# Moving a bias addition from VectorE to GpSimd, and the order of VectorE's work, in the stage between two layers

## The reference

```python
x = x + attn0(xn0) + ffn0(xn0)            # ffn0: u + routed top-2 of 16 experts + shared
xn = (x - mean(x)) / sqrt(var(x) + 1e-5)  # _layernorm, over the last axis, 256 long
# attn1 starts with an rms norm of xn, times sqrt(256), times (gamma + 1)
x = x + attn1(xn) + (xn @ (ternary(weight) * alpha).T + bias)
```

## Time and profile before

| | before |
|---|---|
| median of 3 runs | 3188.59 us (3183.55 to 3188.95) |
| profiled execution | 3183.55 us, span 3181.5 us |
| busy over the span | PE 89%, DVE 68%, POOL 66%, ACT 60% |
| `settle` | 695.6 us (first load issued) to 943.3 us (first instruction of the next stage) |
| L1040 of the first and of the last unit | 707.2 and 928.0 us |

### The profile page before, as it was taken

How to read it: one execution, slowest core, us unless ns; L and a number is a source line. 1 busy time by engine, 2 the same in 40 slices (tenths; PEclk the granted TensorE clock), 3 DMA queues, 4 the chain that set the end, 5 groups by cost and what they waited for, 6 DMA issues and landing times.

```text
span 3181.5 us, 49742 instructions
## 1 busy us (share of the span) xinstructions
PE 2845.0 (89%) x14674; PEld 2191.7 (69%) x14674; DVE 2166.3 (68%) x3533; ACT 1899.3 (60%) x2746; POOL 2093.5 (66%) x1314
## 2 busy tenths in 40 slices
PE   5888848864448999999999999999999999999997
PEld 5788847753335677777777777777777777777775
DVE  7888843338876667677667667676676667667673
ACT  4555422222226777677777777677776777777774
POOL 4777741017744777777777777777777777777775
PEclk8988859985558999999999999999999999999998
DMA  3332125558871222222222232222222232232221
GB/s 120 107 107 89 62 83 163 179 180 264 258 228 43 60 56 69 55 65 73 43 76 55 61 76 48 69 54 69 54 64 73 44 76 57 60 76 50 69 53 46
DMA packets 266850, 281.11 MB, mean 88 GB/s; under 512 B 96754, under 2 KB 205554, under 8 KB 266739
## 3 DMA queue, kind: packets, MB, share of 16 engines
q1 hardware_dynamic: 254452, 246.17, 29.2%
q0 software_dynamic: 12288, 33.57, 3.5%
HBM read 129.67 MB, written 82.31 MB: 67 GB/s over the span
## 4 chain that ended last, share of the span: by engine, by line
PE 66%; DMA 1%; ACT 1%; DVE 1%; POOL 1%; issue 1%; SPq 0%; POOLq 0%; ACTq 0%; DVEq 0%
PE psV_b L1615 7%; PE psV_b L1610 7%; PE psV_b L1611 7%; PE psS_b L1598 7%; PE psS_b L1597 7%; PE psN_b L1583 7%; PE psY_b L1538 4%; PE psX_b L1538 4%; PE psY_b L1539 4%; PE psY_b L1540 4%; PE psX_b L1539 4%; PE psX_b L1540 4%; DMA xT_lo<-xT_lo_dram 1%; POOL pp_lo_b L1328 1%; PE psN_b L1667 0%
## 5 line engine op out<-in xcount | busy, mean ns | idle before, releaser
L1328 POOL TENSOR_TENSOR pp_lo_b<-pf_b,pp_hi_b 128x1024 fp32r<-128x1024 f32 x512 | 1228.7, 2400 | 609.0 <-ACT pp_hi_b L1370 523.0
L1474 DVE TENSOR_REDUCE negmax_b<-psN_b 128x2 fp32r<-128x1024 f32 x512 | 627.0, 1225 | 378.6 <-PE psN_b L1583 371.1
L1365 ACT ACTIVATE pf_b<-psS_b 128x1024 f32<-128x1024 f32 x512 | 525.8, 1027 | 238.7 <-PE psS_b L1598 235.6
L1597 PE MATMUL psS_b<-qA_b,kA_b 128*128 128x512 f32 x1024 | 405.9, 396 | 6.7 <-DVE qB_b L1489 4.8
L1598 PE MATMUL psS_b<-qB_b,kB_b 68*128 68x512 f32 x1024 | 406.3, 397 | 0.0
L1611 PE MATMUL psV_b<-pp_hi_b,vals_lo_b 128*64 128x512 f32 x1024 | 403.4, 394 | 0.0
L1610 PE MATMUL psV_b<-pp_hi_b,vals_hi_b 128*65 128x512 f32 x1024 | 401.8, 392 | 1.5
L1583 PE MATMUL psN_b<-kA_b,qA_b 128*128 128x512 f32 x1024 | 322.6, 396 | 4.6 <-DVE negmax_b L1474 4.5
L1389 ACT ACTIVATE kA_b<-psX_b 64x512 fp32r<-64x512 f32 x256 | 151.7, 593 | 290.1 <-PE psX_b L1540 285.2
L1615 PE MATMUL psV_b<-pp_lo_b,vals_hi_b 128*65 128x512 f32 x1024 | 320.2, 394 | 5.0 <-POOL pp_lo_b L1328 5.0
L1370 ACT ACTIVATE pp_hi_b<-pf_b 128x1024 fp32r<-128x1024 f32 x256 | 271.5, 1061 | 8.1
(11 more groups left out here) (246 smaller groups left out, 6542.4 us busy)
## 6 DMA issues: line engine op xcount, KB each, us to landing
kA_b<-kA_b SPq DMA_DIRECT2D x128, 256.0 KB, 3.2
qB_b<-qA_b SPq DMA_DIRECT2D x128, 256.0 KB, 2.9
inverse_b<-inverse_dram SPq DMA_DIRECT2D x256, 128.0 KB, 3.1
xs_e<-rows_dram SPq DMA_DIRECT2D x144, 128.0 KB, 2.1
results_dram<-ys_e SPq DMA_DIRECT2D x72, 256.0 KB, 2.4
x_a<-x_dram SPq DMA_DIRECT2D x16, 512.0 KB, 4.2
part_dram<-acc_a SPq DMA_DIRECT2D x32, 256.0 KB
acc_s<-part_dram SPq DMA_DIRECT2D x32, 256.0 KB
```

What stands on the lines that cost most here:

```text
L1328: pool.tensor_tensor(pp[1][:, c], pf[:, c], pp[0][:, c].bitcast(F32), ALU.subtract).then_inc(pl_pool, 1)
L1365: a.activation(pf[:, c], psS[:], ACT.Exp).then_inc(exp_act, 1)
L1474: v.tensor_reduce(negmax[:, n.slot(2), 2 * c:2 * c + 2], psN[:], AX.X, ALU.max, negate=True).then_inc(mx_dve, 1)
L1597: pe.matmul(psS[:, t], kA[:, s, keys], qA[:, s], start=True, stop=False)
```

## The change

Three things change in `settle`. The bias addition (result `x1b`) is executed by POOL instead of DVE, after the roots and before the gathers of each unit; the wait for the load of the bias moves from DVE to POOL. POOL computes the two roots in two power instructions of two elements each instead of one of four, and the second reads the variance directly, so that eps is added to two elements only. On DVE `rows_low` is merged into `finish`, which stands where `rows_low` stood: the subtraction, the wait for PE and the base rows of unit u - 1 now come ahead of the factors of unit u. The semaphore counts follow: `SD` is 15 instead of 16, `SP` 4 instead of 2.

```diff
@@ POOL
+            g.wait_ge(const_in, 16)
             for u in range(NU):
                 need(g, s_dve, SD, u, 9)
                 need(g, s_dve, SD, u - 2, SD)
-                g.tensor_tensor(vs[:, u % 2], mv[:, u % 2, :, 1].unsqueeze(1).to_broadcast([P, 2, U]), eps[:], ALU.add).then_inc(s_pool, 1)
+                g.tensor_tensor(vs[:, u % 2, 0], mv[:, u % 2, :, 1], eps[:], ALU.add).then_inc(s_pool, 1)
                 need(g, s_pool, SP, u, 1)
-                g.tensor_tensor(flat2(root[:, u % 2]), flat2(vs[:, u % 2]), flat2(power[:]), ALU.pow).then_inc(s_pool, 1)
+                g.tensor_tensor(root[:, u % 2, 0], vs[:, u % 2, 0], power[:, 0], ALU.pow).then_inc(s_pool, 1)
+                g.tensor_tensor(root[:, u % 2, 1], mv[:, u % 2, :, 1], power[:, 1], ALU.pow).then_inc(s_pool, 1)
+                need(g, o_dve, U, u - 3, U)
+                g.tensor_tensor(x1b[:, u % 3], x1[:, u % 3], fbias_bc[:].unsqueeze(1).to_broadcast([P, U, D]),
+                                ALU.add).then_inc(s_pool, 1)
                 gather(u + 3)
@@ DVE
-            def rows_low(u):
+            def finish(u):
                 if u < 0:
                     return
                 need(v, t_act, 1, u, 1)
+                v.tensor_tensor(flat(xrt[1][:, u % 2]), psT[:, u % 2], flat(xrt[0][:, u % 2]).bitcast(F32),
+                                ALU.subtract).then_inc(t_dve, 1)
+                need(v, s_pool, SP, u, 4)
                 if u >= 2:
                     v.wait_ge(stored[u % 2], 80 * (u // 2))
-                v.tensor_tensor(flat(xrt[1][:, u % 2]), psT[:, u % 2], flat(xrt[0][:, u % 2]).bitcast(F32),
-                                ALU.subtract).then_inc(t_dve, 1)
-
-            def finish(u):
-                if u < 0:
-                    return
                 need(v, f_pe, 1, u, 1)
                 for t in range(U):
                     v.scalar_tensor_tensor(out=base[:, u % 2, t], in0=psF[:, u % 2, t * D:(t + 1) * D], scalar=fac[:, u % 3, 5, t:t + 1],
                                            in1=x1b[:, u % 3, t], op0=ALU.mult, op1=ALU.add).then_inc(o_dve, 1)
 
-            v.wait_ge(const_in, 16)
             for u in range(NU):
...
                     v.bn_aggr(mv[:, u % 2, t], stats[:, u % 2, t]).then_inc(s_dve, 1)
-                rows_low(u - 1)
-                v.tensor_tensor(x1b[:, u % 3], x1[:, u % 3], fbias_bc[:].unsqueeze(1).to_broadcast([P, U, D]),
-                                ALU.add).then_inc(s_dve, 1)
+                finish(u - 1)
                 f = fac[:, u % 3]
-                need(v, s_pool, SP, u, 2)
+                need(v, s_pool, SP, u, 3)
                 v.tensor_tensor(f[:, 0], root[:, u % 2, 0], root[:, u % 2, 1], ALU.mult).then_inc(s_dve, 1)
...
                 v.scalar_tensor_tensor(out=f[:, 4], in0=mv[:, u % 2, :, 0], scalar=-1.0, in1=f[:, 3],
                                        op0=ALU.mult, op1=ALU.mult).then_inc(s_dve, 1)
-                finish(u - 1)
-            rows_low(NU - 1)
             finish(NU - 1)
```

More of the change, by code:

```diff
@@ L906, in settle @@
         power = sb("power", [P, 2, U])
-        eps = sb("eps", [P, 2, U])
+        eps = sb("eps", [P, U])
         acc = sb("acc", [P, 4, U, D])
@@ L927, in settle @@
             "const_in", "const_pool", "s_dve", "s_pool", "x_act", "t_pe", "t_act", "t_dve", "f_pe", "o_dve"))
-        SD = 5 + 2 + 2 + 1 + 6
-        SP = 2
+        SD = 5 + 2 + 2 + 6
+        SP = 4
         def flat(ap):
             return ap.rearrange("p a b c -> p (a b c)")
-        def flat2(ap):
-            return ap.rearrange("p a b -> p (a b)")
         block = ctx.enter_context(nc.Block())
@@ L977, in _ @@
         def _(g):
-            for tile, value in ((power[:, 0], -0.5), (power[:, 1], 0.5), (eps[:, 0], 1e-5), (eps[:, 1], 0.0)):
+            for tile, value in ((power[:, 0], -0.5), (power[:, 1], 0.5), (eps[:], 1e-5)):
                 g.memset(tile, value).then_inc(const_pool, 1)
-            g.wait_ge(const_pool, 4)
+            g.wait_ge(const_pool, 3)
             def gather(u):
@@ L1039, in _ @@
                 need(v, x_act, U, u - 3, U)
+                need(v, s_pool, SP, u - 3, 4)
                 v.tensor_tensor(acc[:, u % 4], acc[:, u % 4], x[:, u % 4], ALU.add).then_inc(s_dve, 1)
@@ L1054, in _ @@
                 need(v, s_dve, SD, u, 7)
-                need(v, s_pool, SP, u - 2, 2)
+                need(v, s_pool, SP, u - 2, 3)
                 for t in range(U):
                     v.bn_aggr(mv[:, u % 2, t], stats[:, u % 2, t]).then_inc(s_dve, 1)
-                rows_low(u - 1)
-                v.tensor_tensor(x1b[:, u % 3], x1[:, u % 3], fbias_bc[:].unsqueeze(1).to_broadcast([P, U, D]),
-                                ALU.add).then_inc(s_dve, 1)
+                finish(u - 1)
                 f = fac[:, u % 3]
-                need(v, s_pool, SP, u, 2)
+                need(v, s_pool, SP, u, 3)
                 v.tensor_tensor(f[:, 0], root[:, u % 2, 0], root[:, u % 2, 1], ALU.mult).then_inc(s_dve, 1)
+                need(v, s_dve, SD, u, 10)
+                v.tensor_scalar(f[:, 1], f[:, 0], 1e-12 * float(D) ** -0.5, None, ALU.max).then_inc(s_dve, 1)
                 need(v, s_dve, SD, u, 11)
-                v.tensor_scalar(f[:, 1], f[:, 0], 1e-12 * float(D) ** -0.5, None, ALU.max).then_inc(s_dve, 1)
-                need(v, s_dve, SD, u, 12)
                 v.reciprocal(f[:, 2], f[:, 1]).then_inc(s_dve, 1)
                 v.tensor_scalar(f[:, 5], f[:, 1], kept.alpha_bc[:, 0:1], None, ALU.mult).then_inc(s_dve, 1)
+                need(v, s_dve, SD, u, 13)
+                v.tensor_tensor(f[:, 3], f[:, 2], root[:, u % 2, 0], ALU.mult).then_inc(s_dve, 1)
                 need(v, s_dve, SD, u, 14)
-                v.tensor_tensor(f[:, 3], f[:, 2], root[:, u % 2, 0], ALU.mult).then_inc(s_dve, 1)
-                need(v, s_dve, SD, u, 15)
                 v.scalar_tensor_tensor(out=f[:, 4], in0=mv[:, u % 2, :, 0], scalar=-1.0, in1=f[:, 3],
                                        op0=ALU.mult, op1=ALU.mult).then_inc(s_dve, 1)
-                finish(u - 1)
-            rows_low(NU - 1)
             finish(NU - 1)
```

## The result

The changed kernel takes 3227.61 us (median of four runs, 3223.29 to 3234.82) against 3186.07 us before (four runs), a ratio of 1.0143 with a 95% interval of 1.0125 to 1.0162: 41.5 us slower. The forecast was 3221, 34.6 us slower, in a range of 3213 to 3243. It was right in sign, and in the cause of the greater part of the loss; it was 7 us short in size.

A forecast was written before the change was run, and what follows sets the result against it. The prediction took settle's loop from low-half rows through PE to base rows as the bound. Factors 31.5, POOL 1.7, collision 1.0 and first roots 0.4 gave +34.6 us; it said 3221 us, range 3213 to 3243.

The forecast's parts named there:

- The loop through PE sets the period: In settle, low-half transposed rows, PE's matmuls, base rows and next sums make the whole 7.12 us unit.
- Factors uncovered, 1.00 us a unit, +31.5: DVE's six factor instructions, formerly covered by PE's time, now follow the base rows: 8.12 us a unit, +31.5 us.
- The gap itself at 2.17: DVE's wait for PE between low-half transposed rows and base rows stays 2.17 us a unit.
- the changed semaphore counts are free: Changed semaphore counts in settle were claimed to cost nothing.
- POOL at 8.18, a tie that costs 1.7: POOL's cycle per unit becomes 8.18 us, tying with DVE's 8.12; +1.7 us over 29 units with gathers.
- Rival B: POOL becomes the bound of settle, its cycle 8.82 to 9.26 us: 3239 to 3252 us; chance 0.25.
- Collision with the addition, once, 1.0 us: POOL's bias addition holds up DVE's factors at the shared SBUF once, then POOL is early enough: +1.0 us.
- DVE's loss gives POOL room: Argument against DVE and POOL colliding in every unit of settle, a rival at about 3260 us; chance 0.05.
- Bias addition worth nothing to DVE: Taking 32 additions, 21.8 us, off DVE saves 0, as they lie inside its wait for PE.
- Not slower (D): The 2.17 us is instruction placement, not PE's need: unit 7.12 us or shorter, down to 3170 us; chance 0.05.

The follow-up runs named there:

- Experiment 1: Kernel before with only the base rows moved ahead of the factors, bias addition still on DVE: 3214.71 us against 3181.89, ratio 1.0109.
- experiment 5: PE multiplies high halves before the low halves are ready: in the kernel before 3175.73 us against 3185.16; in the changed kernel 3217.29 us, ratio 1.0092.
- experiment 2: Kernel before, DVE order kept, with the bias addition and two powers of 2 elements on POOL: 3224.00 us, ratio 1.0135.
- experiment 4: Kernel before, DVE order kept, one power of 4 elements, bias addition on POOL behind the four gathers: 3204.23 us, ratio 1.0057.
- 3: Kernel before, DVE order kept, bias addition on POOL behind the roots, one power of 4 elements: 3211.00 us, ratio 1.0087.

## Why the prediction was nearly right

*The loop through PE sets the period.* Right. Experiment 1 keeps the gap at 2.17 with other contents, experiment 5 shrinks it and with it the unit.

*Factors uncovered, 1.00 us a unit, +31.5.* Right in mechanism: 32.5 in the stage by itself. In the changed kernel the term was mis-sized: the factors measured 1.26, of which 0.17 is the small TENSOR_SCALAR held up by a gather and 0.09 the gap behind the last factor (0.17 for 0.08), 0.06 of that by the wait for POOL; the other 0.03 is in experiment 1 too, where the sum follows the last factor by 0.11. The prediction looked for collisions only between DVE and POOL's addition; it did not look at the gathers, which had met the factors in each unit of the kernel before too, but at their start.

*The gap itself at 2.17.* Short by 0.09 a unit. The text has "the changed semaphore counts are free", and gives the added waits no term. Two more waits, satisfied, cost 0.10 in the kernel before. Together 1.00 + 0.17 + 0.09 + 0.09 = 1.35 of the 1.37 us by which the unit grew; over 31 units the forecast misses 11 us here, less in the first units. With the 1.7 us for POOL that were not paid, this is about the 9.3 by which the stage's 43.9 exceeds the 34.6. The medians differ by 41.5 only, so the forecast came out nearer in them than in the stage, and part of that nearness is luck.

*POOL at 8.18, a tie that costs 1.7.* The cycle was right, 8.16. The cost was not paid, since DVE was slower than forecast and POOL waited for it. Rival B did not happen in the changed kernel; it is what stands next behind DVE's loop, as experiment 5 shows at 8.10.

*Collision with the addition, once, 1.0 us.* Right: 1.22 for 0.16 in the first unit, not again. The text argued that DVE's loss gives POOL room; in the order of before that argument fails, and the collision comes in each unit (experiment 2). There it was no rival of the changed kernel, but it is one reason why undoing the order doesn't rescue the edit; the other is POOL's own length (experiment 4).

*Bias addition worth nothing to DVE.* Right: the 21.8 us of work taken off it are found nowhere as a gain.

*Not slower (D).* Excluded: the gap is 2.17 to 2.27 in the new order whatever DVE does in it, and it shrinks where PE starts earlier.

## What to carry to other kernels

An engine that is busy 89% of a stage need not be its bound: add up one period from instruction to instruction, and see which wait would open if the work beside it were taken away. The work that fills a wait is free and is the last to move; what stands behind the wait is what should be drawn into it, or the wait itself shortened, as by starting PE on the half that is ready (6.80 for 7.12 us a unit). Two engines in a near tie should be looked at together: which of them leads decides which of their instructions meet, and here one late start of some 0.4 us went with 0.17 us more in each unit behind it.

## What the hardware showed that was not expected

- A small TENSOR_SCALAR (2 elements) on DVE takes 0.17 us alone or 0.03 to 0.11 us into a POOL gather, and 0.34 when it starts 0.64 us into one, ending 0.04 us before the gather does. A SCALAR_TENSOR_TENSOR of the same values in the same place takes 0.16.
- A satisfied wait in front of a DVE instruction is not free. One more ahead of the first sum made 0.06 us; two more ahead of the base rows made 0.10 in the kernel before and 0.09 in the changed one, where DVE stands idle for the whole of that gap of 2.26 us. Why is open.
- DVE and POOL released by the same event race, and in these traces POOL won each time: its addition began 0.04 to 0.07 us ahead of DVE's factor (all 32 units of experiment 2 and of 3), which then took 1.22 to 1.25 instead of 0.16. Beside POOL's power of 4 elements, DVE's addition with two SBUF inputs took its 0.68 us unchanged.
